# Softmax on 160 selected score columns, no mask product, one input for the head, and a quarter of the differences on VectorE

## The reference, cut to what matters

```python
for inds in inds_list:                       # 4 sort orders
    neigh = gather(feats, inds)              # window of 10 neighbours
    gf = concatenate([broadcast(center), neigh - center], axis=-1)
...
qh = x16.reshape(B * N, k, nheads, headdim)  # k = 10, 8 heads of 64
scores = einsum('bihd,bjhd->bhij', qh, qh) / sqrt(headdim)
attn = softmax(scores, axis=-1)
out = einsum('bhij,bjhd->bihd', attn, qh)
fused = out @ W_lin.T + b_lin
```

## Time and profile before

| what | value |
|---|---|
| time, median of 3 runs | 1002.33 us (1000.74 to 1005.09) |
| the profiled execution | 1002.12 us, span 1000.5 us |
| granted TensorE clock, mean | 0.997 |
| busy: PE, PEld | 958.8 us (96%), 734.6 us (73%) |
| busy: DVE, ACT, POOL | 735.7 us (74%), 467.5 us (47%), 449.5 us (45%) |
| cloud layer 1, first to last mask product | 501.67 to 662.98 us |
| cloud layer 2, first to last mask product | 714.08 to 899.88 us |

### The profile page before, as it was taken

How to read it: one execution, slowest core, us unless ns; L and a number is a source line. 1 busy time by engine, 2 the same in 40 slices (tenths; PEclk the granted TensorE clock), 3 DMA queues, 4 the chain that set the end, 5 groups by cost and what they waited for, 6 DMA issues and landing times. The chain is left out here.

```text
span 1000.5 us, 38062 instructions
## 1 busy us (share of the span) xinstructions
PE 958.8 (96%) x15968; PEld 734.6 (73%) x15968; DVE 735.7 (74%) x1932; ACT 467.5 (47%) x765; POOL 449.5 (45%) x408
## 2 busy tenths in 40 slices
PE   3899999999999999999989999999999999999998
PEld 1699878696969687765977777768866666665695
DVE  6698747956657483797968888978788888887410
ACT  6343324141423323212377777774576767674010
POOL 1101211630212202020299999960798888886000
PEclk9999999999999999999999999999999999999999
DMA  8997797877887796566213222231222222221660
GB/s 339 406 407 280 257 326 268 332 285 279 309 301 295 255 350 232 184 259 254 92 39 73 66 71 65 70 78 66 68 68 64 53 62 55 60 56 41 252 253 22
DMA packets 58794, 182.42 MB, mean 182 GB/s; under 512 B 9193, under 2 KB 10969, under 8 KB 58330
## 3 DMA queue, kind: packets, MB, share of 16 engines
q1 hardware_dynamic: 55058, 172.03, 49.2%
q0 software_dynamic: 2432, 8.42, 2.4%
q10 hardware_dynamic: 1224, 0.81, 0.4%
HBM read 154.45 MB, written 1.61 MB: 156 GB/s over the span
## 5 line engine op out<-in xcount | busy, mean ns | idle before, releaser
L558 PEld LDWEIGHTS ps<-hT,ring 128*128 128x128 f32 x2304 | 258.3, 192 | 6.7 <-issue 6.5
L558 PE MATMUL ps<-hT,ring 128*128 128x128 f32 x2304 | 260.1, 276 | 0.0
L2040 POOL TENSOR_TENSOR X<-sortedT,ring 128x960 f16 (+1 forms) x84 | 158.8, 1891 | 21.0 <-PE ps L1614 20.9
L991 POOL TENSOR_TENSOR y_y<-y_z,sgate 128x512 f32<-128x512 f32 x16 | 20.1, 1273 | 192.6 <-DVE y_z L922 192.6
L2065 POOL TENSOR_TENSOR PP<-S,PP 128x480 f16<-128x480 f32 x86 | 100.0, 1163 | 5.3 <-ACT PP L1808 5.3
L1633 PE MATMUL ps<-PT,ring 128*64 128x120 f16 x2752 | 97.4, 222 | 5.0 <-DMA PT<-P_turned 2.3
L591 PE MATMUL ps<-wt,y_n 128*128 128x512 f32 x224 | 99.4, 596 | 1.5 <-DVE xs L914 1.5
L1633 PEld LDWEIGHTS ps<-PT,ring 128*64 128x64 f16 x2752 | 84.3, 110 | 18.4 <-issue 8.0
L1808 ACT CAST PP<-S 128x480 f16<-128x480 f32 x86 | 67.0, 779 | 60.5 <-POOL S L2058 60.5
L2058 POOL TENSOR_TENSOR S<-S,den 128x480 f32<-128x480 f32 x86 | 88.9, 1033 | 3.7 <-DVE den L1935 3.7
L821 DVE SCALAR_TENSOR_TENSOR xc<-xpad,parg,xc 128x128 f32<-128x128 f32 x192 | 59.2, 371 | 42.3 <-ACT xc L705 41.1
(11 more groups left out here) (330 smaller groups left out, 1555.9 us busy)
## 6 DMA issues: line engine op xcount, KB each, us to landing
ring<-in_w_in SPq DMA_DIRECT2D x36, 2048.0 KB, 9.4
wt<-in_w_out SPq DMA_DIRECT2D x14, 2048.0 KB, 7.7
PT<-P_turned SPq DMA_DIRECT2D x332, 64.0 KB, 2.0
ring<-in_w SPq DMA_DIRECT2D x8, 1024.0 KB, 12.1
ctx_chunks<-in_ctx SPq DMA_DIRECT2D x4, 1024.0 KB, 10.9
krow<-keys_scratch POOLq DMA_DIRECT2D x8, 512.0 KB, 7.0
mchunk<-in_mask_t POOLq DMA_DIRECT2D x8, 512.0 KB, 8.1
ring<-in_w_out SPq DMA_DIRECT2D x2, 2048.0 KB, 8.2
```

Source lines behind the costliest of these rows:

```text
L558: mm = nc.tensor.matmul(ps[:, bank, j * T:(j + 1) * T], weights[:, j, kc * P:(kc + 1) * P], k.hT[:, kc, :], start=kc == 0, stop=kc == KC - 1)
L2040: ins = gp.tensor_tensor(fcopy(c.X[u][:, 0, 0:1], full(cnt)), fcopy(c.fsT[:, 0, bass.ds(it * STEP, 1)], trio(start, cnt, 1)), fcopy(c.fTr[ ...
```

## The change

**Cloud layers.** The mask product and its constants go. The scores of a block are written so that columns of the same third lie together, and DVE picks for each partition the third that is its own window: three operations on 160 columns, each with a per-partition factor of `own` (1 for the own third, 0 for others). Maximum, subtraction, exponential and sum then work on 160 columns (`E`) instead of 480. `denominators` gains a product of the reciprocals with `own` (48 columns), and POOL's `normalise` spreads `E` times that to 480 columns, so that foreign thirds become zero. PE does `rows` ahead of `scores`, and both wait for the last of the three picks (`s_read`). `shift` waits for `normalise` of two steps ago instead of `low_part`. In layer 1, for steps 2 to 41, DVE computes the last of the four quarters of `differences` (`last_quarter`) and POOL three.

**The head.** One DMA from SP brings scalars, two mixer parameters and the coordinates, already turned by the host; the six DMAs of ACT, PE's transpose and ACT's copy go, and the addition of the row term moves from DVE to ACT.

```diff
 stage_quantised_product
             sp.dma_start(k.x[:, :], dr["x"]).then_inc(s_x, 16)
+            sp.dma_start(k.head_in[:, :], dr["head_in"]).then_inc(s_sc, 16)
...
-            v.wait_ge(s_sc, 64)
+            v.wait_ge(s_sc, 16)
...
-            nc.vector.tensor_scalar(k.x[:, :], k.x[:, :], rowb[:, 3:4], None, ALU.add).then_inc(s_q1, 1)
...
-            for i, name in enumerate(("L0_xattn_x1_scale", "L0_xattn_x1_zp", "L0_xattn_x2_scale", "L0_xattn_x2_zp")):
-                act.dma_start(sc[:, i:i + 1], dr[name].partition_broadcast(P)).then_inc(s_sc, 16)
...
+            act.wait_ge(s_row, 5)
+            nc.scalar.activation(k.x[:, :], k.x[:, :], ACT.Identity, bias=rowb[:, 3:4], scale=1.0).then_inc(s_row, 1)
...
 stage_cloud_layer
+        shared = lambda it: layer == 1 and (not isinstance(it, int) or 2 <= it < STEPS - 1)
+        def difference(eng, it, u, first, count, trios):
+            dims = lambda row, step, last: [[row, count], [TRIO * step, trios], [step, TRIO], last]
+            return eng.tensor_tensor(fcopy(c.X[u][:, first, 0:1], [[STEP // TRIO * 32, count], [32, trios], [WIN, TRIO], [1, WIN]]),
+                                     fcopy(c.fsT[:, first, bass.ds(it * STEP, 1)], dims(c.W, 1, [1, WIN])),
+                                     fcopy(c.fTr[:, first, bass.ds(it * STEP + LEAD, 1)], dims(N, 1, [0, WIN])), ALU.subtract)
+        def normalised(wait, eng, it, u):
+            if after(it, 2):
+                wait.wait_ge(s_lo, t0 + it - 1)
+            eng.tensor_tensor(c.S[u][:, :, :].rearrange("p s (w j) -> p s w j", j=WIN), fcopy(c.E[u][:, 0, :], [[WIN, 2 * SLOTS], [0, TRIO], [1, WIN]]),
+                              fcopy(c.den_own[u][:, 0, :], [[TRIO, 2 * SLOTS], [1, TRIO], [0, WIN]]), ALU.mult).then_inc(s_P, 1)
...
             def scores(it, ph):
-                for r in range(2):
-                    half = slice(r * C, (r + 1) * C)
-                    nc.tensor.matmul(ps[:, S_BANK + r, 0:COLS], c.rows_u[half, :], c.cols_v[half, :, :].rearrange("p s i -> p (s i)"),
-                                     start=True, stop=False)
...
             def rows(it, ph):
+                pe.wait_ge(s_X, t0 + it + 1)
+                if shared(it):
+                    pe.wait_ge(s_Xv, it - 1)
+                if after(it, 1):
+                    pe.wait_ge(s_read, t0 + it)
...
+                rows(*lagged(0))
                 scores(*lagged(0))
-                rows(*lagged(0))
...
             def shift(it, ph):
                 v.wait_ge(s_S, t0 + it + 1)
                 if after(it, 2):
-                    v.wait_ge(s_lo, t0 + it - 1)
+                    v.wait_ge(s_P, t0 + it - 1)
+                third = lambda w: ps[:, S_BANK:S_BANK + 2, w * SLOTS * WIN:(w + 1) * SLOTS * WIN]
+                vec.tensor_scalar(E, third(0), own[:, 0:1], None, ALU.mult).then_inc(s_sel, 1)
+                v.wait_ge(s_sel, 2 * t0 + it * 2 + 1)
+                vec.scalar_tensor_tensor(out=E, in0=third(1), scalar=own[:, 1:2], in1=E, op0=ALU.mult, op1=ALU.add).then_inc(s_sel, 1)
+                v.wait_ge(s_sel, 2 * t0 + it * 2 + 2)
+                vec.scalar_tensor_tensor(out=E, in0=third(2), scalar=own[:, 2:3], in1=E, op0=ALU.mult, op1=ALU.add).then_inc(s_read, 1)
+                v.wait_ge(s_read, t0 + it + 1)
+                vec.tensor_reduce(c.mx[u][:, :], c.E[u][:, :, :], AX, ALU.max).then_inc(s_max, 1)
                 v.wait_ge(s_max, t0 + it + 1)
+                vec.tensor_tensor(c.E[u][:, :, :], c.E[u][:, :, :], fcopy(c.mx[u][:, :], [[1, 2 * SLOTS], [0, WIN]]), ALU.subtract).then_inc(s_sub, 1)
...
             def denominators(it, ph):
+                v.wait_ge(s_den, 3 * t0 + it * 3 + 2)
+                vec.tensor_tensor(c.den_own[u][:, :, :], fcopy(c.den[u][:, :], [[1, 2 * SLOTS], [0, TRIO]]),
+                                  fcopy(c.own[:, :], [[0, 2 * SLOTS], [1, TRIO]]), ALU.mult).then_inc(s_den, 1)
+            def last_quarter(it, ph):
...
+                v.wait_ge(s_S, t0 + it - 1)
+                difference(vec, it, ph % 2, 3, 1, STEP // TRIO).then_inc(s_Xv, 1)
             def step(it, lagged):
                 denominators(*lagged(0))
+                last_quarter(*lagged(-2))
...
             def differences(it, ph):
-                    pool.wait_ge(s_xt, t0 + it - 1)
+                    pool.wait_ge(s_S, t0 + it - 1)
+                ins = difference(gp, it, u, 0, 3 if shared(it) else 4, cnt)
```

More of the change, by code:

```diff
@@ L1329, in cloud_constants @@
         gp.memset(whole[(slice(None),) * len(whole.shape)], 0.0).then_inc(c.filled, 1)
[L1330 to L1331 removed]
+    gp.memset(c.own[:, :], 1.0).then_inc(c.filled, 1)
     gp.iota(c.iota[:, :], [[1, N]], base=0, channel_multiplier=0, allow_small_or_imprecise_dtypes=True).then_inc(c.filled, 1)
[L1333 removed]
+    pool.wait_ge(c.filled, 11)
     for q in range(4):
         gp.memset(c.blocks[32 * q:32 * q + 32, 32 * q:32 * q + 32], 1.0).then_inc(c.filled, 1)
[L1336 to L1353 removed]
+    pool.wait_ge(c.filled, 15)
+    for q in range(4):
+        rows = c.own[32 * q:32 * q + 32, :]
+        gp.affine_select(out=rows, in_=rows, compare_op=ALU.is_ge, fill=0.0, base=0, pattern=[[-WIN, TRIO]], channel_multiplier=1).then_inc(c.shaped, 1)
+    pool.wait_ge(c.shaped, 4)
+    for q in range(4):
+        rows = c.own[32 * q:32 * q + 32, :]
+        gp.affine_select(out=rows, in_=rows, compare_op=ALU.is_ge, fill=0.0, base=WIN - 1, pattern=[[WIN, TRIO]], channel_multiplier=-1).then_inc(c.shaped, 1)
+    pool.wait_ge(c.shaped, 8)
 def weight_products(nc, pe, k, layer):
@@ L1387, in __init__ @@
         self.den = [sb(f"den{u}", [P, 2 * SLOTS]) for u in range(2)]
+        self.E = [sb(f"E{u}", [P, 2 * SLOTS, WIN]) for u in range(2)]
+        self.den_own = [sb(f"den_own{u}", [P, 2 * SLOTS, TRIO]) for u in range(2)]
         self.PT = k.PT
@@ L1585, in scores @@
                     return
-                pe.wait_ge(s_X, t0 + it + 1)
-                if after(it, 1):
-                    pe.wait_ge(s_sub, t0 + it)
                 X = c.X[ph % 2]
-                for r in range(2):
-                    half = slice(r * C, (r + 1) * C)
-                    nc.tensor.matmul(ps[:, S_BANK + r, 0:COLS], c.rows_u[half, :], c.cols_v[half, :, :].rearrange("p s i -> p (s i)"),
-                                     start=True, stop=False)
                 for slot in range(SLOTS):
@@ L2093, in host_layout @@
     d = {"x": a["x"].reshape(T, D), "ctx_4096": a["ctx_4096"]}
-    for n in ("L0_xattn_x1_scale", "L0_xattn_x1_zp", "L0_xattn_x2_scale", "L0_xattn_x2_zp"):
-        d[n] = a[n]
     w = a["L0_attn_in_proj_w"].reshape(-1, P, KC, P)
```

84 lines of the change are left out of this document (32 added, 52 removed).

## The result

The changed kernel takes 1038.74 us (median of 4 runs, 1038.33 to 1040.71), the kernel before 1002.22 us in the same comparison: ratio 1.0364, 95% interval 1.0344 to 1.0383. It is 36.5 us slower. The prediction was 1007 us with a range up to 1022, so it had the sign of the likeliest group right and the size wrong. The profiled execution took 1038.47 us, its span is 1036.6 us, the mean granted clock 0.99 (0.997 before).

What follows compares the result with a forecast made beforehand. Before, POOL bounds layer 1 and PE layer 2; after, DVE both. Layer 1 +12.2, layer 2 -4.5, head -1.8, end of layer 1 -0.8 make +5.1 us on 1002.12: 1007 us, range 992 to 1022.

Steps and rivals of the forecast that it cites:

- the likeliest group: Whole kernel: the outcome slower, above 1007.3 us, given chance 0.46, against 0.36 within and 0.18 faster.
- The interface between DVE and POOL: Cloud layers: DVE operations with two SBUF inputs share it with POOL's SBUF reads; the first holds it to its end.
- the wait that the sum leaves out: Cloud layers: DVE's subtraction waits for POOL's differences, 0.13 us a step in layer 1 (0 to 0.3), 0.04 in layer 2.
- Rival B: Cloud layers: DVE doesn't get in between POOL's operations; about 5.4 us a step in both, 1088 us, chance 0.14.
- a mean wait above 0.15 us in layer 1: Layer 1, DVE's subtraction: the sign said to decide for DVE not getting in between POOL's operations.
- A mean above 0.8 us: Subtraction's mean time: above this the prediction is wrong and DVE doesn't get in between POOL's operations; 0.4 to 0.6 expected.
- Idle time of DVE of 0.3 us in a step of layer 1: Layer 1: if DVE still has this much idle time in a step, the prediction is wrong.
- Half of rival B: Cloud layers: half the loss from DVE not getting in between POOL's operations, giving 1045 us.
- DVE's sum in layer 1: Layer 1: DVE's operations of one step added from start to start, 4.07 us, against 3.87 us a step before.
- The first eight steps: First steps of both layers: put at nothing; if cover is gone, 0.3 us in each of ten, 3 us.
- the 37: Steps counted in each cloud layer: +0.33 us each in layer 1, -0.12 us each in layer 2.
- The head: Kernel start: one DMA brings the scalars earlier and an addition goes to ACT; -1.8 us (bounds -0.8 and -2.7).

Runs made afterwards that it cites:

- the run with both edits: Changed kernel with the maximum in PSUM and the first pick on ACT, ahead of ACT's copy of the rows: 998.56 us, ratio to the kernel before 0.9962.
- the run without the hold: Changed kernel with the maximum kept in PSUM, so the subtraction has one SBUF input: 1020.56 us, ratio to the kernel before 1.0180.

## Why the prediction was wrong

**Right.** DVE is the bound in both layers. The prices hold: the picks 376 and 384 ns (0.36 and 0.385 predicted), the maximum 0.32 and the sum 0.28 us (0.30 for both), the subtraction 0.32 where it is free (0.33). PE without its mask product needs 4.32 us in layer 2, as the run with both edits shows. The interface between DVE and POOL was named as the danger.

**The step that failed** is the one on the wait that the sum leaves out. Counted from the product with `own`, it put the subtraction of layer 1 at 2.6 us, in the middle of POOL's differences, let it wait for their end at 2.9, and took 0.13 us a step for that; for layer 2 it took 0.04. In the trace the subtraction of a good step comes at 2.81 us (600.09 to 602.90) and the low part at 2.90. There it isn't held at all, and in layer 2 for 0.05 to 0.15 us. But the working treated the meeting as a cost that grows with the overlap, while it is a threshold 0.09 us away, with 0.8 us of hold behind it. And it gave DVE no reason to be late, although the kernel before shows one: its DVE had 0.26 us of idle time by issue every fourth step of layer 1, hidden under POOL's bound:

```profile
594.35 0.41 DVE L1893 BATCH_NORM_STATS2 stats<-ps 128x240 f32 x1 [0.26 <-issue]
```

At the turn of the changed kernel the subtraction comes at 3.12 us (604.37 to 607.49), behind the low part. By the prediction's own schedule that slip would have been harmless, 2.6 + 0.22 against 2.9: the miss needs the 0.21 us by which its sum was short as well. Rival B had the price of a miss, 5.4 us a step; what was missing was to ask how often it happens. It happens at each of the 8 turns in a layer. In layer 1 that is 8 x (18.21 - 4 x 4.28) = 8.7 us; in layer 2, where two good steps take 4.45 and 4.54 us and a turn 19.09, 8 x (19.09 - 4 x 4.49) = 9.0 us, slips included.

Of the signs in the text, a mean wait above 0.15 us in layer 1 was met: the subtraction's mean there is 0.58 us, 0.26 more than when it is free. A mean above 0.8 us was not (0.62 over both layers), and stood too high. Idle time of DVE of 0.3 us in a step of layer 1 was met (4.55 - 4.25), but most of it is the 0.03 to 0.04 us between operations that wait for each other, which the sum counts, so that sign was set too tight. Half of rival B, 1045 us, was the nearest figure in the prediction, by luck: nothing in it says how often the miss comes.

**Terms that were mis-sized.**
- DVE's sum in layer 1: 4.28 us against 4.07. Of the 0.21 us, 0.13 lie between the product with `own` and the quarter, 0.25 us from start to start where 0.12 were taken; the statistics that follow that product in layer 2 start 0.13 us behind it. The quarter computes its addresses from the step's number; whether that is the reason was not tested. The rest is 0.01 to 0.04 in each of the other operations. In 32 loop steps it makes 6.7 us. Layer 2 has 4.41 in the run without the hold, against 4.36.
- The turn of the loop by itself, put at nothing: with the maximum in PSUM, where no subtraction is held, a turn still costs about 0.34 us in layer 1 and 0.60 in layer 2, 2.7 and 4.8 us in all.
- The first eight steps, put at nothing except for those among the 37: +3.8 us in each layer. With the maximum in PSUM they are +1.7 and +1.4, so more than half of it is the hold again; the subtraction takes 0.94 and 1.6 us there. What is left in layer 2 still has a hold in it: there the product with `own` takes 0.9 to 1.16 us in five steps. The prediction gave 3 us for it as the price of a lost cover, for both layers together.
- The head: 3.0 us up to the first subtraction in place of 1.8. `x` itself came 1.6 us earlier, here and in the run with the head alone (4.51 and 4.57 against 6.09), where ACT issued no DMAs beside it; whether these DMAs are the reason was not tested by themselves.
- Between the layers +2.5 us and behind them -2.0, both put at nothing. Their causes were not tried.

**What the runs show of the cause.** Taking the second SBUF input away gives 18 us back; adding 0.19 us of work costs 48 us; taking 0.37 us of work away costs nothing or 2 us; taking 0.41 away gives 0.28 us a step of layer 1 while the subtraction can be held, and 0.43 once it can't. A sum of work can't give these four. Of the 36.5 us, 18 are the hold, by the run with the maximum in PSUM. The other 17.5 (that run's span is 1018.0 us) lie nearly all in layer 1: first to last subtraction 180.21 against 162.40 us, +17.8. Of these, 13.1 are DVE's sum (4.28 against 3.87 us in 32 steps), 2.7 the turns, 1.7 the first steps and 0.3 the last. Layer 2 has 188.42 against 186.15, +2.3; the start gives 2.9 back, and the rest is +0.3.

## What to carry to other kernels

Where two engines share an interface and one of them issues back to back, an operation that arrives near the other's hand-over is priced with both outcomes: look at how far it stands from the hand-over, and at the slips of the engine's own loop, even those that another bound hides today. Before moving work, count the SBUF inputs of each DVE operation that runs beside POOL; a small operand in PSUM can be worth more than the operation itself. And when a kernel is bound by such a hold, less work shows no gain, so remove the hold first and judge the rest after it.

## What was not expected of the hardware

- A held subtraction of 160 columns ends 0.18 us behind POOL's end (608.57 against 608.39, 874.70 against 874.52), the product with `own`, 48 columns, 0.06 us behind it (603.99 against 603.93): less than either takes when free, as if part of the operation were done while it is held; no run separates the two.
- The turn of a loop costs DVE mostly 0.22 us of issue in layer 1 and 0.30 to 0.47 in layer 2, with nothing waited for.
- A loop body of eight steps in place of four brought DMAs on an instruction queue, 9 packets and 0.15 MB in 40 us, and a stop of PE of 1.70 us in the middle of its score products; the turns of layer 1 took 7.8 to 8.6 us from subtraction to subtraction in place of 4.6.
- PE's granted clock fell to 0.50 at three of the eight turns of layer 1, behind a wait of 1.38 us at the one shown, and not in the loop of layer 2, where PE waited 1.34 us at the turn shown. With the maximum in PSUM it stayed at 1.00 in both layers.
